# A rebuilt last stage of a four-stage image block: chunked top-8 routing, packed expert products, stores issued from GpSimd's queue

## What is computed

```python
def _L1_ffn_ref(x, gate_w, gate_b, weight1, weight2):
    B, S, D, E, H, O, K = (256, 1024, 64, 32, 256, 64, 8)
    logits = jnp.einsum('bsd,ed->bse', x, gate_w) + gate_b
    probs = jax.nn.softmax(logits, axis=1)
    vals, idx = jax.lax.top_k(probs.transpose(0, 2, 1), K)
    topv = vals.transpose(0, 2, 1)
    ...
    pooled = jnp.einsum('bked,bke->bed', gathered, topv)
    h = jnp.concatenate([pooled.transpose(1, 0, 2), ones], axis=-1)
    h = jax.nn.gelu(jnp.einsum('ebd,edh->ebh', h, weight1), approximate=False)
    h = jnp.concatenate([h, ones], axis=-1)
    out = jnp.einsum('ebh,eho->ebo', h, weight2)
    ...
    outputs = outputs.at[jnp.arange(Bn)[:, None], flat_idx].add(weighted)

t = t + _L1_ffn_ref(_ln_t(t), L1_ffn_gate_w, L1_ffn_gate_b, L1_ffn_weight1, L1_ffn_weight2)
```

## Time and profile before

| | |
|---|---|
| median of three runs | 8588.15 us |
| profiled execution, its own time | 8588.41 us |
| span of its instructions | 8586.6 us |
| `phase_c` in it | from 8107.7 us to the end, 479 us |
| granted TensorE clock, mean of the span | 0.820 of 2.4 GHz |
| DVE busy in the span | 79% |

### The profile page before, as it was taken

How to read it: one execution, slowest core, us unless ns; L and a number is a source line. 1 busy time by engine, 2 the same in 40 slices (tenths; PEclk the granted TensorE clock), 3 DMA queues, 4 the chain that set the end, 5 groups by cost and what they waited for, 6 DMA issues and landing times. The chain is left out here.

```text
span 8586.6 us, 102988 instructions
## 1 busy us (share of the span) xinstructions
PE 6282.9 (73%) x30668; PEld 2512.8 (29%) x30668; DVE 6791.2 (79%) x7924; ACT 4293.2 (50%) x5876; POOL 5185.6 (60%) x1723
## 2 busy tenths in 40 slices
PE   6888888888876777676776767777777777777455
PEld 3444444444431222222222222222222222222133
DVE  3555555555547999999999999999999999999634
ACT  1222222222225666666666666666666666666400
POOL 0000000000007999999999999999999999999500
PEclk8889889898977888888888888888888888888666
DMA  1111111111114655656556566565655656565553
GB/s 33 41 42 41 45 39 43 42 40 45 41 36 172 206 196 194 209 184 205 197 195 208 184 202 198 194 211 185 209 192 195 207 190 211 187 202 197 143 154 125
DMA packets 513971, 1253.45 MB, mean 146 GB/s; under 512 B 170085, under 2 KB 172297, under 8 KB 513673
## 3 DMA queue, kind: packets, MB, share of 16 engines
q1 hardware_dynamic: 513417, 1252.41, 45.2%
q0 software_dynamic: 512, 0.53, 0.0%
HBM read 943.30 MB, written 231.21 MB: 137 GB/s over the span
## 5 line engine op out<-in xcount | busy, mean ns | idle before, releaser
L1185 DVE TENSOR_TENSOR_SCAN b_h<-b_a,b_h 128x448 f32<-128x448 f32 x3584 | 3673.9, 1074 | 101.6 <-ACT b_a L1114 95.3
L1023 POOL TENSOR_TENSOR b_h<-b_h,b_ct 128x1792 f32<-128x1792 f32 x896 | 3571.1, 3989 | 279.6 <-DVE b_h L1185 265.8
L1114 ACT ACTIVATE b_a<-b_dts,decay 128x441 f32<-128x441 f32 x3584 | 2225.4, 629 | 1587.2 <-DVE b_h L1185 1560.3
L1035 POOL MEMSET b_seq<- 128x938 f32 x2 | 1.7, 880 | 2496.6 <-POOLq L798 2496.6
L1175 DVE TENSOR_TENSOR b_h<-b_dus,b_b 128x896 f32<-128x896 f32 x1344 | 1434.7, 1068 | 62.0 <-DMA b_dus<-d_dtu 60.6
L1282 PE MATMUL b_b<-b_rows,spread_b 16*128 16x512 f32 (+1 forms) x1792 | 567.6, 652 | 886.4 <-DVE b_h L1175 885.3
L1009 POOL TENSOR_TENSOR b_h<-b_dus,b_bt 128x896 f32<-128x896 f32 x448 | 933.9, 2085 | 44.8 <-DMA b_bt<-d_rows 28.1
L1290 PE MATMUL b_y<-b_h,fold 128*32 128x512 f32 (+1 forms) x7168 | 951.4, 658 | 8.1 <-POOL b_h L1023 8.1
L495 DVE TENSOR_TENSOR a_xg<-a_xd,a_pb 128x784 f32<-128x784 f32 x512 | 495.3, 967 | 519.4 <-PE a_pb L609 517.3
L1251 PE MATMUL b_w<-b_seq,w_conv 128*128 128x384 f32 (+1 forms) x896 | 557.4, 786 | 12.6 <-DMA b_seq<-b_seq 12.6
L1243 PE MATMUL b_w<-b_u,wx 128*64 128x512 f32 x448 | 361.1, 961 | 212.5 <-DVE b_dt L1207 212.5
(11 more groups left out here) (211 smaller groups left out, 8586.9 us busy)
## 6 DMA issues: line engine op xcount, KB each, us to landing
b_bt<-d_rows SPq DMA_DIRECT2D x448, 448.0 KB, 6.0
b_ct<-d_rows SPq DMA_DIRECT2D x448, 448.0 KB, 3.9
b_dts<-d_dt SPq DMA_DIRECT2D x448, 448.0 KB, 5.7
b_dus<-d_dtu SPq DMA_DIRECT2D x448, 448.0 KB, 6.2
a_xd<-a_xn SPq DMA_DIRECT2D x256, 196.0 KB, 3.4
d_dt<-b_dt SPq DMA_DIRECT2D x112, 448.0 KB, 2.5
d_dtu<-b_soft SPq DMA_DIRECT2D x112, 448.0 KB, 2.6
b_seq<-b_seq SPq DMA_DIRECT2D x112, 234.0 KB, 6.4
```

The source lines that it names most:

```text
L1023: nc.gpsimd.tensor_tensor(two, two, ct[t // 4 % 2][:].unsqueeze(1).broadcast_to([P, 2, TB]), ALU.mult).then_inc(hc_done, 2)
L1114: a(steps(bank(aa, k)), steps(half(dts[t % 4], k)), ACT.Exp, scale=decay[:, t % 4, t // 4:t // 4 + 1]).then_inc(a_done, 1)
L1185: v.tensor_tensor_scan(half(hh[t], k), bank(aa, k), half(hh[t], k), 0.0, ALU.mult, ALU.add).then_inc(h_done, 1)
```

## The change

`phase_c` is written anew; `phase_a` and `phase_b` keep their code (their line numbers move by one). To make room, the constants that only they use are freed before `phase_c` (`mid`).

- **Loads.** `lt` exists twice. Each is loaded in four column parts; for the first tile SP issues the upper 64 rows and ACT the lower 64. SP then issues the weights, the second tile's logits and all 56 loads of chunks; there are 8 chunk slots `xs`, and the load into a slot waits for the store out of it (slots 6 and 7 also serve ACT as scratch, and wait for its last sum).
- **Search.** `find` takes the 8 largest of each part as it lands and then of those 32. `match_replace` writes to a bf16 array `chosen`. ACT makes the sum of the exponentials chunk by chunk into scratch (`sums`), and once `chosen` is there the exponentials in place (`gates`); DVE zeroes them chunk by chunk (`gate`) just ahead of the chunk's use.
- **Experts.** The pooled vectors, four columns, are the stationary operand and 256 columns of weights move; four experts go to the four column groups of PE (output partitions 0, 32, 64, 96). Each product is followed by one that adds the bias (a one-hot of 32 rows against `w1b`). The result is turned back by 16 products with the identity (`turn_hidden`), multiplied by `w2` (`products`), and gathered into rows by 9 products (`gather_rows`). ACT moves PSUM results that DVE moved before, and fills `mix`.
- **Order.** There is one block for both tiles. The second tile's search runs on DVE after the first tile's pooling; its experts run on PE between chunks 16 and 27 of the first tile.
- **Chunks.** DVE adds into the loaded slot, and POOL issues the store from there. The loops are written out, 56 chunks in one stream.

```diff
-                lt = sb("l", [R, HW])
-                gt = sb("g", [R, HW])
+                lt = each("l", [R, HW])
+                chosen = sb("chosen", [R, HW], BF16)
...
-                xs = [sb(f"x{i}", [P, CK]) for i in range(2)]
-                ys = [sb(f"y{i}", [P, CK]) for i in range(2)]
+                xs = [sb(f"x{i}", [P, CK]) for i in range(SLOT)]
...
+                        def load(n):
+                            _, k, c = place_of(n)
+                            if n in (LEAD + 1, SLOT - 1):
+                                sp.wait_ge(exp_ready[1], NK)
+                            if n >= SLOT:
+                                sp.wait_ge(stored[n % SLOT], 16 * (n // SLOT))
+                            sp.dma_start(xs[n % SLOT][:], x3[:, k * HW + c * CK:k * HW + (c + 1) * CK]).then_inc(x_loaded[n % SLOT], 16)
...
+                        def store(n):
+                            _, k, c = place_of(n)
+                            pool.wait_ge(y_ready, n + 1)
+                            nc.gpsimd.dma_start(out_v[k, :, c * CK:(c + 1) * CK], xs[n % SLOT][:]).then_inc(stored[n % SLOT], 16)
...
+                        sums(0, 0, NK)
+                        a(p8[0][:], top[0][:], ACT.Exp, bias=neg[0][:]).then_inc(e8_ready[0], 1)
+                        gates(0, 0, 4)
+                        pooled(0)
+                        gates(0, 4, 9)
+                        gelu(0, 0)
+                        gelu(0, 1)
+                        turned(0)
+                        gates(0, 9, NK)
+                        act.wait_ge(neg_ready[1], 1)
+                        act.wait_ge(exp_ready[0], NK)
+                        sums(1, 0, 5)
+                        outputs(0)
+                        mixer(0)
+                        sums(1, 5, NK)
...
+                        find(0)
+                        take(0)
+                        pooling(0)
+                        find(1)
+                        for c in range(2):
+                            gate(0, c)
+                        for n in range(NT * PER):
+                            if n < NK - 2:
+                                gate(0, n + 2)
+                            if n == NK:
+                                pooling(1)
+                                take(1)
+                            if PER - 2 <= n < PER + NK - 2:
+                                gate(1, n - PER + 2)
+                            dve.wait_ge(y_prod, n + 1)
+                            dve.wait_ge(x_loaded[n % SLOT], 16 * (n // SLOT + 1))
+                            v.tensor_tensor(xs[n % SLOT][:], py[n % 2][:, 0:CK], xs[n % SLOT][:], ALU.add).then_inc(y_ready, 1)
...
+                        def hidden(t, half):
+                            pe.wait_ge(px_ready[t], 1)
+                            if half:
+                                pe.wait_ge(gelu_ready[t], half)
+                            by_expert = pool_x[t][:].rearrange("d (b e) -> d e b", e=EC)
+                            for q in range(NQ // 2 * half, NQ // 2 * (half + 1)):
+                                at = q % (NQ // 2) * HID
+                                for g in range(4):
+                                    x = 4 * q + g
+                                    h = slice(C * half, C * half + C)
+                                    dst = ph[32 * g:32 * g + IMG, at:at + HID]
+                                    mm(dst, by_expert[h, x, :], w1[h, x % (EC // 2), :], start=True, stop=False)
+                                    last = mm(dst, by_e[:, :, x], w1b[:], start=False, stop=True)
...
+                            if n % PER == 0:
+                                pe.wait_ge(mix_ready[t], IMG)
+                            if n % PER < NK:
+                                pe.wait_ge(g_ready[t], c + 1)
+                            if n >= 2:
+                                pe.wait_ge(y_ready, n - 1)
...
+                            if n == 16:
+                                turn(1)
+                            if n == 17:
+                                hidden(1, 0)
+                            if n == 19:
+                                hidden(1, 1)
+                            if n == 21:
+                                turn_hidden(1)
+                            if n in (23, 25):
+                                products(1, NQ // 2 * (n // 25), NQ // 2 * (n // 25 + 1))
+                            if n == 26:
+                                gather_rows(1)
```

More of the change, by code:

```diff
@@ new lines, in phase_c @@
+                pt, hid_p, pr = pm[:, 0:R], pm[:, R:R + 8 * NQ * IMG], pm[0:R, R + 8 * NQ * IMG:R + 8 * NQ * IMG + C]
+                w_loaded, zeroed, places = sem("wl"), sem("zero"), sem("place")
+                l_loaded = [sems(f"ll{t}", LC) for t in range(NT)]
+                neg_ready, exp_ready, e8_ready, chain, idx_ready, gathered, taken, e_ready, g_ready, pool_ready = (
+                    sems(n) for n in ("neg", "exp", "e8", "chain", "idx", "gath", "taken", "ex", "gr", "pool"))
+                tr_ready, px_ready, h_ready, gelu_ready, ht_ready, hid_ready, o_ready, ot_ready, pr_ready, mix_ready = (
+                    sems(n) for n in ("tr", "px", "h", "gelu", "ht", "hid", "o", "ot", "pr", "mix"))
@@ new lines, in mixer @@
+                                a(mix[t][q, b // 2, C * (b % 2):C * (b % 2) + C], pr[q, :], ACT.Copy, scale=rec[t][q, 0:1]).then_inc(mix_ready[t], 1)
+                        for c in range(LC):
+                            load_logits(act, 0, c, 1)
+                        act.wait_ge(zeroed, ZEROS)
+                        act.wait_ge(neg_ready[0], 1)
+                        sums(0, 0, NK)
+                        a(p8[0][:], top[0][:], ACT.Exp, bias=neg[0][:]).then_inc(e8_ready[0], 1)
+                        gates(0, 0, 4)
@@ L1570, in program @@
         phase_b()
+        mid.close()
         end_phase()
```

414 lines of the change are left out of this document (238 added, 176 removed).

## The result

The changed kernel takes 8467.94 us (median of four runs, 8435.74 to 8489.55), the kernel of before beside it 8584.35 (four runs, 8579.07 to 8592.71): a ratio of 0.986 (95% interval 0.982 to 0.990), 116 us less. The forecast was 8433, in a range of 8375 to 8515. The time is in the range and the sign is right, but the gain is three quarters of the 155 us claimed, and two large terms were wrong in opposite directions: the experts' products took 60.5 and 53.9 us a tile, not 28, and the DMA engines moved 403 GB/s among the last chunks, not 333. The profiled execution (8435.74, span 8434.0) meets the forecast span of 8431 almost exactly, by luck: its last stage started 39 us earlier than in the profile of before, at 8068.8 and not 8107.8, behind the same code.

What follows compares the result with a forecast made beforehand. It took the last stage to be bound by latency in series. First add 8231, then 34, 17, 77, 68 and the end gave span 8431, with 1.8 us of profile offset 8433; range 8375 to 8515.

Steps and rivals of the forecast that it cites:

- first add: Start of the chunks' adds on DVE: forecast at 8231 on the old trace's clock, against 8246 before.
- chunks 0 to 13: Tile 0's first 14 chunks: loads and stores queued behind tile 1's sums, 8.3 MB at 333 GB/s, 34 us.
- DVE's block: Tile 1's pooling 3.4 plus marking 13.2 on DVE: 17 us in which the adds stand.
- chunks 14 to 27 with tile 1's experts: PE's chunk products 32 us, experts and their followers 28 + 5 + 8 + 3, scaling 1.1: 77 us.
- chunks 28 to 55: Last 28 chunks: DVE 45, PE 64, DMA 66 us at 333 GB/s; taken as 68 us.
- end: Behind the last add: last store issued by POOL 1.25 us plus landing 2.5, reaching 8431.
- the one way to a slower kernel: POOL's chunk stores: slower than before if each takes over 6.3 us; chance of slower 0.04, nearly all POOL.
- the term of 28 us for the experts' 64 products: PE's 64 expert products of 256 columns per tile: one at a time at 2.4 GHz or two at 1.2, 28 us.
- The prediction's own sign of being wrong: At the start of tile 0's chunks: the forecast is wrong if the first add waits for PE past 8245.
- the serial rival: PE's experts stay serial at 1.2 GHz, 54 us a tile, 74 us more in all: 8507; chance 0.18.
- 52 in all: Tile 0's PE chain before its first chunk: experts 28, Gelus and table load, turning 5, products 8, rows 3, copies, handovers.
- three limits near-equal: Among the last 28 chunks DVE 45, PE 64 and DMA 66 us were called near-equal limits.

Runs made afterwards that it cites:

- e6: Changed kernel with only tile 1's marking pass on DVE moved from ahead of the 15th add to ahead of the 19th; 8443.61 us, ratio 0.986, stage 349.6 us.
- e5: Changed kernel with only ACT reordered: tile 0's last five exponentials and tile 1's first five sums moved ahead of the first Gelu; 8438.04 us, ratio 0.985.
- e9: Changed kernel with SyncE issuing tile 1's logits only after tile 0's eight gathers have landed; 8447.41 us in one run, stage 358.6 us.
- e11: Changed kernel with only the last eight of its 56 stores issued by SyncE instead of GpSimd; 8468.16 us in one run, stage 361.6 us.
- e4: Changed kernel with all chunk stores back on SyncE's queue, in turn with the loads; 8448.53 us, ratio 0.986, stage 357.8 us.
- after: The changed kernel itself, against the kernel of before; 8467.94 us, ratio 0.986, stage 365.2 us.
- e12: Version with all repairs, SyncE's stores and 40 idle products, plus twelve of tile 0's exponentials, not four, ahead of the pooled rows on ACT; 8326.17 us, ratio 0.972.
- e10: Version with all repairs and SyncE's stores, plus 40 unread products of 128 columns on PE before tile 0's pooled rows; 8339.78 us, ratio 0.973.

## Why the prediction was right or wrong

Step by step, counted from the stage's start (the forecast's clock less 8107.7):

| step | forecast | measured |
|---|---|---|
| negated maximum of tile 0 | 37.7 | 33.1 |
| marking done | 64.9 | 60.2 |
| rows pooled | 68.3 | 72.1 |
| DVE ready with tile 1's search | 117.3 | 105.7 |
| first add | 123.3 | 164.2 |
| chunks 0 to 13 | 34 | 27 |
| DVE's block | 17 | 16.4 |
| chunks 14 to 27 with tile 1's experts | 77 | 87.7 |
| chunks 28 to 55 | 68 | 60.4 |
| end | 4 | 9.5 |
| stage | 323 | 365 |

**What was right.** The stage was bound by latency in series, and most of that is gone: two preludes of 277 us are one of 164, while the chunks take 191.5 us and took 195.6. That this comes of running the two tiles side by side is read from these stretches; no run takes the overlap back by itself. The search went as told (DVE's whole passes at 13.2 us, the quarters of the first at 3.4, the logits a little faster than the 34 us left in place); DVE's block was sized to 0.6 us, and e6 shows that it was in the path. GpSimd's stores did not limit, at 0.54 us against the 1.25 taken, so the one way to a slower kernel did not occur. The Trainium skill's warning (SBUF — State Buffer, SBUF: two separate sides) is of 3.1 us beside a DVE copy. No run here shows that: the stores stood beside adds and gates and took 0.54 in the mean.

**The step that failed** is the term of 28 us for the experts' 64 products, "one at a time at the higher level or two at a time at the lower": they ran one at a time, and mostly at the lower. Measured: 60.5 in tile 0, 27.7 + 26.2 = 53.9 in tile 1. The prediction's own sign of being wrong came true with it: on its clock the first add came at 8272, waiting for PE, past the 8245 named. The time is in the range because the range reaches to the serial rival and because errors cancelled (below). The text had the case, *Serial at 1.2 GHz*, at 54 us and a chance of 0.18. The Trainium skill's rule that a change of tiling mode drains TensorE (TensorEngine Tiling (Array Packing), Tiling Modes, Key Properties) stood for it. The text set the case aside because in the earlier trace rows a one-row product starts 0.31 us before its neighbour with a record of 0.37. That is an overlap of 0.06 us: it says that little is lost at a change of rows, not that four products run side by side across one. The step was 32 us too low in tile 0 and 26 in tile 1, where the chunks and small products around it, at 34 us and not 49, made up for part. Within the rival the mechanism was right, the size 6 us short in tile 0; its whole, 8507, is a stage of 397 us, too long by those small products and the chunks. The sum's other slips were small: the terms of "52 in all" add up to 51.

**Waits that were not in the sum.** ACT's order: the text saw the five sums ahead of the outputs' copy and had them over by 8213.5, but not the table load and five exponentials (6.0 us) ahead of them, which begin only when PE's turned rows are copied: 8.35 us (e5). The gathers: landing 2.4 by the earlier trace rows, in truth 10.6, since they now share the engines with tile 1's logits: 8.7 us (e9). The end: 9.5, not 4 (e11 and e4).

**What cancelled.** DMA moved 403 to 420 GB/s where 333 was the highest row seen, so the last 28 chunks took 60 and not 68 us (the text called three limits near-equal there; DVE's, 45, was not), and the first 14 were held by DVE at 2.0 us a chunk (27, not 34; DVE was busy for 25.3 of them). Errors of +41, +11 and +5.5 against -7, -1 and -8 make the +42 of the table. Most of the miss was hidden in the profile: from the start of 8107.8 on which the forecast was built, this stage would end at 8473, not 8431, but the stages ahead were 39 us shorter in that run. In the median they were only some 7 shorter (8467.94 less 1.8 and the stage is 8101), so 35 of the 42 show there.

## What to carry to other kernels

Before costing small matrix products as packed, look at what stands next to each in the queue: pad or reorder neighbours to the same number of rows; that was worth 81 of 365 us here. When latency is hidden by running two chains side by side, go through every in-order engine that serves both and ask what of the other chain stands ahead of the path's next copy, gather or pass: three such places held 6.8 us (e5), 15.2 (e6) and 6.2 (e9), each measured by itself. Measure a late stage from its own start when the stages ahead of it vary by more than the edit is worth.

## What the hardware showed that was not expected

- Alternating products of 64 and 32 rows, with four columns of weights and 256 moving ones, ran singly at 0.944 us; the same order with 64 rows throughout ran four in 0.855, at the same granted clock of 0.50.
- The granted clock fell from 1.00 to 0.50 while PE was busy without a gap with products of four weight columns (after, both halves of tile 1; e12, tile 0). It rose from 0.50 to 1.00 during forty products of 128 columns (e10).
- Loads and stores together moved up to 420 GB/s at a DMA share of 1.02.
- A store issued by GpSimd took 0.54 us of that engine; from its queue the program ended 7.0 us after the last data, from SyncE's 2 to 2.7.
